# Attention of a fused cross-attention and expert kernel: eight score products in one run, one shared unit a step

## What is computed

```
q, k, v = layernorm(x) @ Wq + bq, ctx @ Wk + bk, ctx @ Wv + bv     # 16 heads of 16
attn    = softmax(clip(q k^T / 4, -10000, 10000))                  # 8 x 16 x 512 x 512
x       = x + tanh(g_xattn) * ((attn @ v) @ Wo + bo)
logits  = layernorm(x) @ gate_weight^T                             # 8 experts
gates   = logits * (logits >= the 6144th smallest of all 32768)
x       = x + tanh(g_ffn) * sum over e of gates_e * (gelu(x' @ w1_e + b1_e) @ w2_e + b2_e)
```

## Time and profile before

| | |
|---|---|
| profiled execution | 2204.5 us |
| its span | 2202.7 us |
| runs | 2200.15, 2202.37, 2203.65 us |
| TensorE busy in the span | 2003.1 us, 91% |
| VectorE busy | 1359.9 us, 62% |
| ScalarE busy | 719.7 us, 33% |
| GpSimd busy | 230.9 us, 10% |
| granted TensorE clock, mean | 0.958 |

### The profile page before, as it was taken

How to read it: one execution, slowest core, us unless ns; L and a number is a source line. 1 busy time by engine, 2 the same in 40 slices (tenths; PEclk the granted TensorE clock), 3 DMA queues, 4 the chain that set the end, 5 groups by cost and what they waited for, 6 DMA issues and landing times.

```text
span 2202.7 us, 29673 instructions
## 1 busy us (share of the span) xinstructions
PE 2003.1 (91%) x9252; PEld 1446.8 (66%) x9252; DVE 1359.9 (62%) x2389; ACT 719.7 (33%) x1206; POOL 230.9 (10%) x227
## 2 busy tenths in 40 slices
PE   3758999999975999899999989999998998999998
PEld 3643333333334788788778878877887886888887
DVE  7748888888836675645555465465456456454554
ACT  2224766666751222222222222222221222222222
POOL 5210111001114000200110020020002002000000
PEclk9877999999986999999999999999999999999999
DMA  3753322222201000100100010010001001000010
GB/s 108 242 190 111 81 77 73 71 79 78 62 30 60 0 28 18 48 10 15 38 20 14 10 48 14 10 48 14 10 13 49 10 10 47 14 10 15 29 43 34
DMA packets 80059, 103.39 MB, mean 47 GB/s; under 512 B 25986, under 2 KB 44164, under 8 KB 80004
## 3 DMA queue, kind: packets, MB, share of 16 engines
q1 hardware_dynamic: 80004, 102.71, 15.6%
HBM read 76.34 MB, written 26.08 MB: 46 GB/s over the span
## 4 chain that ended last, share of the span: by engine, by line
PE 63%; DVE 6%; ACT 0%; issue 0%; DVEq 0%; ACTq 0%
PE ps_y L1840 31%; PE ps_h L1826 31%; DVE h_lo L2047 3%; DVE h_hi L2043 2%; DVE candidate L2086 0%; ACT gelu L1946 0%; DVE w_hi L1986 0%; DVE gated L2112 0%; DVE out_T_acc L2117 0%; DVE w_lo L1988 0%; PE ps_h L1876 0%; DVE gate L2076 0%; DVE gate L2058 0%; PE ps_h L1908 0%; DVEq L1995 0%
## 5 line engine op out<-in xcount | busy, mean ns | idle before, releaser
L1946 ACT ACTIVATE gelu<-ps_h,b 128x512 f32<-128x512 f32 x512 | 352.0, 688 | 1153.6 <-PE ps_h L1826 1047.2
L2043 DVE CAST h_hi<-gelu 128x512 fp32r<-128x512 f32 x512 | 254.3, 497 | 601.5 <-ACT gelu L1946 601.2
L1840 PE MATMUL ps_y<-h_hi,w_hi 128*128 128x512 f32 x1024 | 410.3, 401 | 42.6 <-DVE h_lo L2047 42.6
L1826 PE MATMUL ps_h<-x_hi,w_hi 128*128 (+1 forms) x1024 | 413.5, 404 | 9.2 <-DVE w_lo L1988 9.2
L2047 DVE TENSOR_TENSOR h_lo<-gelu,h_hi 128x512 fp32r<-128x512 f32 x512 | 408.0, 797 | 16.5
L1826 PE MATMUL ps_h<-x_lo,w_hi 128*128 (+1 forms) x1024 | 411.0, 401 | 0.0
L1826 PE MATMUL ps_h<-x_hi,w_lo 128*128 (+1 forms) x1024 | 410.3, 401 | 0.0
L1840 PE MATMUL ps_y<-h_hi,w_lo 128*128 128x512 f32 x1024 | 408.0, 398 | 0.0
L1840 PE MATMUL ps_y<-h_lo,w_hi 128*128 128x512 f32 x1024 | 407.8, 398 | 0.0
L898 DVE TENSOR_REDUCE low<-ps_s 128x1 f32<-128x512 f32 x512 | 322.0, 683 | 39.8 <-PE ps_s L755 37.8
L1840 PEld LDWEIGHTS ps_y<-h_hi,w_hi 128*128 128x128 f32 x1024 | 195.3, 191 | 96.2 <-DVE h_lo L2047 48.3
(11 more groups left out here) (209 smaller groups left out, 1406.7 us busy)
## 6 DMA issues: line engine op xcount, KB each, us to landing
gate<-gates_scratch SPq DMA_DIRECT2D x64, 256.0 KB, 3.3
q_st<-q_scratch SPq DMA_DIRECT2D x64, 132.0 KB
k_scratch<-k_hl SPq DMA_DIRECT2D x32, 256.0 KB
q_scratch<-q_hl SPq DMA_DIRECT2D x32, 256.0 KB
k_st<-k_scratch SPq DMA_DIRECT2D x64, 128.0 KB
w_raw<-in_w1T SPq DMA_DIRECT2D x8, 1024.0 KB, 4.9
w_raw<-in_w2T SPq DMA_DIRECT2D x7, 1024.0 KB, 5.2
v_scratch<-v_out SPq DMA_DIRECT2D x8, 544.0 KB
```

The costliest lines, as they stand in the source:

```text
L1826: mm = pe.matmul(ps_h[:, j % RING, :], w[:, k, at], x[:, k, bass.ds(c * SEQ, SEQ)], start=(i == 0), stop=(i == len(parts) - 1))
L1840: mm = pe.matmul(ps_y[s][:, d, :], w[:, j, at], h[:, j % RING, :], start=(j == 0 and i == 0), stop=(j == HT - 1 and i == 2))
L1946: act.activation(gelu[:, j % GELUS, :], ps_h[:, j % RING, :], ACT.Gelu_apprx_tanh, bias=b1[p][:, j:j + 1]).then_inc(gelu_done, 1)
L2043: dve.tensor_copy(h_hi[:, j % RING, :], gelu[:, j % GELUS, :]).then_inc(h_hi_done, 1)
```

## The change

In `batch` on TensorE the eight score products of a step are issued in one run; unit (g, k, 0) follows them, then the V products, then unit (g, k, 1). Four units move in `SHARED`, so that 14 of the 16 steps have one unit and (1,0) and (1,1) two, all but three after the V products. On VectorE the taking of unit (g, k, 0) goes behind the second pair of minima. On ScalarE unit (g, k, 0) is taken after the exponentials of heads 2 and 3, and `copy_out` goes behind both.

```diff
 SHARED = {
-    (0, 0, 1): ("low", 0, 1), (0, 1, 0): ("out", -1, 3), (0, 1, 1): ("rows", -1, 0),
-    (0, 2, 1): ("rows", -1, 1), (0, 3, 1): ("y", -1, 0), (1, 0, 1): ("low", 0, 2),
+    (0, 0, 1): ("low", 0, 1), (0, 1, 1): ("out", -1, 3), (0, 2, 1): ("rows", -1, 0),
+    (0, 3, 1): ("rows", -1, 1), (1, 0, 0): ("low", 0, 2), (1, 0, 1): ("y", -1, 0),
     (1, 1, 0): ("y", -1, 1), (1, 1, 1): ("out", 0, 0), (1, 2, 1): ("x2T", -1, 0),
     (1, 3, 1): ("x2T", -1, 1), (2, 0, 1): ("low", 0, 3), (2, 1, 1): ("out", 0, 1),
     (2, 2, 1): ("xnT", -1, 0), (2, 3, 1): ("xnT", -1, 1), (3, 0, 1): ("low", 1, 0),
-    (3, 1, 0): ("out", 0, 2), (3, 1, 1): ("logits", -1, 0), (3, 3, 0): ("pick", -1, 0),
+    (3, 1, 1): ("out", 0, 2), (3, 2, 1): ("logits", -1, 0), (3, 3, 0): ("pick", -1, 0),
 }
@@ TensorE, batch(b)
-                        if exists(b):
-                            scores_T(b, g, k, 0)
-                        if more:
-                            scores(*ahead, k, 0)
-                        if exists(b):
-                            scores_T(b, g, k, 1)
-                        if more:
-                            scores(*ahead, k, 1)
+                        for j in range(GROUP):
+                            if exists(b):
+                                scores_T(b, g, k, j)
+                            if more:
+                                scores(*ahead, k, j)
+                        shared(b, SHARED.get((g, k, 0)))
                         if exists(back[0]):
                             probs_v(*back)
-                        shared(b, SHARED.get((g, k, 0)))
-                        if exists(b):
-                            scores_T(b, g, k, 2)
-                        if more:
-                            scores(*ahead, k, 2)
-                        if exists(b):
-                            scores_T(b, g, k, 3)
-                        if more:
-                            scores(*ahead, k, 3)
                         shared(b, SHARED.get((g, k, 1)))
@@ VectorE, batch(b)
-                        take_unit(b, (g, k, 0))
                         if more:
                             lows(*ahead, k, 1)
+                        take_unit(b, (g, k, 0))
@@ ScalarE, batch(b)
                         if (g, k) != (0, 0):
                             take_unit(b, STEPS[STEPS.index((g, k)) - 1] + (1,))
+                        if exists(b):
+                            exps(b, g, k, (2, 3))
+                        take_unit(b, (g, k, 0))
                         back = group_after(b, g, -1)
                         if k == 0 and exists(back[0]):
                             copy_out(*back)
-                        if exists(b):
-                            exps(b, g, k, (2, 3))
```

## The result

| | before | changed |
|---|---|---|
| median of the runs beside each other | 2203.01 us | 2225.86 us |
| lowest, highest (four runs each) | 2200.15, 2207.11 | 2223.84, 2226.68 |
| profiled execution, its span | 2204.5, 2202.7 | 2226.7, 2224.9 |

The ratio is 1.0101, with a 95% interval of 1.0083 to 1.0119: slower by 22.9 us at the medians.

What follows compares the result with a forecast made beforehand. No engine is full; a ring of product, reader, freed bank, next product bounds attention. 6 x 3.4 + 3.2 = 23.6 us on 2204.5 gives 2228.1 profiled, so 2226 us median; 8 in 10 range 2207 to 2238.

Steps and rivals of the forecast that it cites:

- (1,0): Attention step, group 1, step 0: `low` waits for `rows` on ScalarE until 2.15, then V products and `y`; 5.25 us.
- (1,1): Attention step, group 1, step 1: the second `y` waits for the first to be taken, 0.8 us; ends at 6.04.
- The trip of the fourth product: In each score run, the fourth `scores` product waits for the first's bank, freed by its minimum: start at 1.31 us.
- one-unit step: Attention step with one unit behind the V products: 2.71 us + unit, 3.29 with four transposes, some 0.4 more.
- takings: VectorE or ScalarE work on a unit's result, now a step later; (2,2), (2,3), (3,0) wait for it: 3.86, 3.60, 3.31.
- (1,3): Attention step, group 1, step 3: VectorE comes 0.98 us late, the 64th product needs the second minimum; 4.30 us.
- `low` steps: Attention steps (0,0) and (2,0), whose unit `low` costs 0.3 us: 3.00 us each.
- `logits`: Unit of step (3,2), four products of 512 columns: taken as 1.14 us between bounds 0.9 and 1.9; step 3.85.
- Batch 0: First batch of attention, with no late units: 47.8 against 47.74 us, so no change.
- The slow clock: Batches 4, 5, 6 each have a short 1.2 GHz stretch costing 1.2 us; three kept. Rival of more stretches: chance 0.24.
- The faster rival: Trip hidden in attention: steps 2.3 us + unit, 0.4 less each, 48 us off, 2178 us; chance 0.09.
- What would show it: Attention signs: one-unit steps 3.3 us, TensorE's waits for minima largest, middle batches 60 to 61 us, batch 0 unchanged.

Runs made afterwards that it cites:

- e1: The kernel before with only the changed kernel's order of products on TensorE; unit table, taking places and `copy_out` stay: 2245.72 us, ratio 1.0199.
- e4: The changed kernel with each row minimum taken over 256 of the 512 keys: 2202.19 us, ratio 1.0002.
- e3: The changed kernel with the fourth pair of score products behind the V products: 2248.17 us, ratio 1.0225.
- e5: e1 with `copy_out` behind the exponentials of heads 2 and 3: 2223.33 us, ratio 1.0081.
- e2: The kernel before with the new `SHARED` table, ScalarE taking unit (g,k,0) ahead of exponentials 2 and 3: 2205.17 us, ratio 1.0021.
- e10: The kernel before with only `copy_out` moved behind the exponentials of heads 2 and 3: 2206.02 us, ratio 1.0007.
- e6: e3 with unit (g,k,0) taken ahead of the second pair of minima and ahead of exponentials 2 and 3: 2229.06 us, ratio 1.011.
- e9: The changed kernel with layernorm normalisations at (2,0) and (2,1), and the high half of `xnT` copied before the exponentials: 2218.58 us, ratio 1.0083.
- e8: The changed kernel run and profiled once more, nothing edited: 2231.53 us.

## Why the prediction was right, and where it wasn't

The forecast was 2226 us and slower; measured are 2225.86. The hit to a fraction of a microsecond is luck, since errors of 3 to 5 us cancel in it, as the fourth point says; the mechanism is not.

- **The trip of the fourth product: shown.** Predicted 1.31 for the product, 1.73 for the V products, 3.29 for a one-unit step; measured 1.32, 1.74 and 3.31. e1 has it with nothing but the new order, and e4 moves the fourth `scores` product from 1.32 to 1.27 with shorter minima. e3 takes the fourth pair out of the run, and its plain steps fall to between 2.6 and 3.2. The predicted "some 0.4 us more for each one-unit step" holds in full in (0,2), 2.90 to 3.31; (1,2) and (2,1) had 3.12 and 3.15 before and pay 0.2, and (2,3) and (3,0), bound by takings in both kernels, pay nothing. By e5 and e2 the new order with the late copy costs 2.6 us a batch and the table 0.9.
- **The steps, one by one.** (1,0) 5.25 predicted, 5.36 measured; (1,1) 6.04, 6.06; (1,3) 4.30, 4.27; (2,2) 3.86, 3.83; (2,3) 3.60, 3.60; (3,0) 3.31, 3.31; (3,1) 3.66, 3.65; (3,2) 3.85, 3.85; (3,3) 4.17, 4.20 at full clock; `low` steps 3.00, 2.92. The sum is 60.5, as predicted. One term came out by a guess: `logits` was put at 1.14 and measured 1.13, but the bounds given for it don't hold. Two thirds of `y` (1.93) are 1.29 and not 0.9, and in the trace the four `logits` instructions have 512 columns where the eight of `y` have 256, so that four against eight is not half the work. Why `logits` is cheaper than `y` is not shown.
- **Batch 0 was mis-sized**: 49.6 us, 48.9 in the second profile, not 47.8; that is 1.8 and 1.0 more than in the two profiles before. I had 2.7 for its step (0,1), which is 4.17 and 3.72, with the clock still low from the stage ahead (0.93 in the batch), and had been 3.55 and 3.72 in the old order too: the old total already held that, my sum of new steps didn't. The run's own cost shows in (1,2) and (2,2), 2.7 us each where the old order had 2.2.
- **By terms** attention was to cost +23.6 and cost +27.0: batches 1 to 6 +22.6 for +20.4, batch 0 +1.8 for nothing, batch 7 +2.6 for +3.2. Of the 22.6, about 20.7 are the steps at full clock and 1.9 the two slow stretches more. The stage ahead happened to be 5.5 us shorter in that execution, and what follows attention 0.7 longer, which gives the 22.2 by which the profiled executions differ. So the forecast was 3.4 too low in attention and nearly 5 too high outside it. Measured against the repeated profiles (2204.22 and 2231.53), the change costs 27 us, and the forecast is 4 short.
- **`copy_out`: right by itself, wrong as a part.** "Its going gains nothing by itself" holds in the old order (e10). I didn't see that the new order needs it: left in its place, it costs 22 us more (e1 against e5). Nor did I see the V products that wait for a late copy in the old order (e10).
- **The slow clock: mis-sized.** I kept three stretches. There were five and four. They begin in (3,3), before the change in (0,0), and cost 1.1 us each (batches 1 to 6 take 368.7 us, six batches at full clock 363.1). The other kernels with eight or six products in a run (e1, e3, e5, e6, e9) have four to nine within attention, those with the old order none to three. But e4, which has the new order, has none. The Trainium skill's rule on bank cycling ("TensorE: Matmul & The Clock Gate", section "A second HAM failure mode: psum-queue depth-cycling") points the right way; but e4 has the same run of eight products, with holds nearly as long. That the idle of the run makes the clock fall is not shown.
- **The faster rival** needed a batch of 54.1 us, which the busy times allow. The latencies don't: its one-unit steps would be 2.9 us, and they are 3.31 in the changed kernel and in e1. The Trainium skill says that a change of tiling mode drains TensorE ("TensorEngine Tiling (Array Packing)", section "Key Properties"). Whether fewer changes gave anything back here is not shown: in the run the third pair follows the second after 0.24 us and the second the first after 0.35, but no change of mode lies between either two, and whatever is saved there lies inside the hold.
- **What would show it** had two wrong signs. TensorE's waits for minima are not the largest in the list (2.2 us in batch 3, against 6.8 for exponentials), since the wait begins at the exponentials. And batch 0 is not unchanged.

## What to carry to other kernels

With three banks a kind and four products a step, ask for each product which work stands between it and the one that held its bank, and compare with the whole trip: here 0.56 us to the reader's start, 0.75 from there to the next product in the bank, 1.31 us in all. Grouping like instructions takes that cover away, though every engine has time to spare. When TensorE's work moves, the readers' order must move with it: `copy_out` in its old place cost 22 us under the new order, and in its new place 0.9 us a batch under the old one. The gain may lie elsewhere: moving a layernorm one step earlier, with one copy ahead of the exponentials, brought 12 us, spreading the units none.

## What the runs showed of the hardware

- A waited pair of half-array products starts in two pieces 0.09 to 0.13 us apart, and what follows comes 0.42 us behind the second (the changed kernel and e4); an unhindered pair before the V products is followed after 0.33 (the kernel before).
- A row minimum over 256 of 512 values takes 419 ns instead of 683, and 0.34 instead of 0.60 us in a full queue (e4).
- The same program's projection stage took 185.4 and 191.1 us in two executions, with VectorE busy 122 and 128 us (the changed kernel and e8).
